# Edge blocks that begin at whole tiles: 860 tile gathers in place of 1004, groups that share tiles, and a ring of 44 places

## The chip, the cores and the metric

The kernel runs on one core of a Trainium2 chip. The time is device microseconds of one execution. TensorE (PE), VectorE (DVE), ScalarE (ACT), GpSimd (POOL) and SyncE (SP) are the core's engines; each runs its own instructions in order, and they wait for one another on semaphores.

## The reference

6250 nodes with 256 features and 100000 edges (`src`, `dst`). Three parts follow each other. The edge part is a graph attention layer, the mix part a transformer block with linear attention, and the last part a mixture of six experts of which each row takes two.

```
Wh = x @ W + b                                  # 6250 x 256
e  = leaky_relu(fs[src] + fd[dst], 0.2)         # fs, fd: Wh by a vector, one number per node
w  = softmax of e over the edges with one src
h  = relu(sum over a src's edges of w * Wh[dst])
x1 = x + linear attention of layernorm(x);  mix = x1 + W2 gelu(W1 layernorm(x1)) (1024 wide)
out = experts of the sum of both parts (router, top 2 of 6)
```

## The kernel before

The rows are cut into 50 blocks of 125 source rows (NT, R). From 0 to 440 us the kernel makes the projections and ranks the edges by block of rows (a counting sort of edges on chip); from 440 to 722 us it writes the sorted edges to `sorted_slots` in memory while the linear attention runs beside it (in `attend`), a stretch in which VectorE has the most to do. At 722 to 738 us the slots are read back (SP), turned (PE) and split by VectorE into `idx_tab`, the node to gather for each slot, and `row_tab`, its source row within the block (lines 839 to 843).

Then comes the edge loop, 738 to 2081 us. A tile is 128 edges, one per partition; a group is GT = 4 tiles, and a group's edges all belong to one block of rows. Before, each block of rows is padded to whole groups, so there are NG = 251 groups and 1004 tiles. GpSimd issues one indirect DMA per tile (line 1212), which gathers 128 rows of 258 floats (Wh and the destination term) from `wh_table` into the buffer `gath`, a ring of RG = 10 groups; it may refill a group's places when TensorE has summed it (`p_main`). Per group:

- DVE `shifted` (1234) waits for the group's gathers, `mark` (1241, four times) makes the one-hot matrix of each tile from `row_tab`, PE `turn` (1434) transposes it, DVE `group_peak` (1251) takes the maximum per row, and five operations on 125x1 numbers keep the running maximum.
- ACT `divide` (1365 to 1370) splits the new maximum into three bf16 parts, `spread` (1353) makes the transposed one-hot, PE `fetch` (1444) hands each edge its row's numbers, and DVE `score_sum`, `score_leaky`, `score_less_max` (1291 to 1305) give the exponents.
- ACT `apart` (1384, four times) and `weigh` (1393, four times) make the weights' matrix, PE `total` (1453) sums weights by gathered rows, DVE `gather_up` (1315) adds it into the block's accumulator `acc_mem` after the rescaling by ACT `rescale` (1376).

The function `together` (line 92) writes the order of every engine out by hand: a slot holds each listed stage once, for the group that lies the given number of slots back, as here for ACT and PE:

```
together(act, roots, [(3, divide), (2, spread), (3, apart), (3, rescale), (4, weigh)], feed)
together(pe, [(5, total), (3, fetch)], feed, [(0, turn), (2, load_block)])
```

Ten slots (PER) make one chunk of 250 rows of the feed-forward network, whose work (`feed`) stands in fixed slots: the sum and the layer norm's statistics on DVE in slot 0 and its root on ACT (295) in slot 1, ACT's `hidden` (1406) in slots 3 to 6, PE's `hidden` (1472) in slots 2 to 5 and `ff` (1483) in slots 6 to 9. Twenty slots are one pass of a loop. After it the experts run to the end at 2609 us.

The block number of a group is a word of the table `group_block`, which PE, DVE and ACT each load into a register once per group (1427, 1252, 1360); with it they address `own_all`, `fr_c` and the accumulator.

## Time and profile before

| | |
|---|---|
| median of 3 runs | 2607.07 us (2606.63 to 2610.53) |
| the profiled execution, its own time | 2610.57 us |
| its span | 2608.9 us |
| mean granted TensorE clock | 0.891 |
| busy over the span: PE, DVE, ACT, POOL | 2048.0, 1857.1, 1579.6, 1353.8 us |
| gathers (1212) | 1004, from 737.9 to 2051.4 us |

Busy time of the whole span mixes stages with different limits; the stretch that matters to an edit is the one in which it stands. A wait is put down to what ended it last. "Issue" is time in which an engine waited for nothing that the profile shows.

### The profile page before, as it was taken

The numbers are of one execution on the slowest core, as the hardware profiler recorded it, in microseconds if no ns is written. First come the engines' busy times: TensorE is split into PE (matmuls) and PEld (weight loads), VectorE is DVE, ScalarE is ACT, GpSimd is POOL, SyncE is SP. The second block draws the span as 40 slices with busy tenths as digits, with TensorE's granted clock in tenths as the row PEclk, the third lists the DMA queues.
The fourth block names the chain that finished last, engine by engine and source line by source line (L and its number), as shares of the span: only waits on it lengthen the run. The fifth ranks groups of instructions, "written<-read, shape, count | busy, mean of one in ns | idle before, by whom it ended". The sixth has DMA issues, their size and how long they took to land. (4 is left out here: it accounts for less than half of the span.)

```text
span 2608.9 us, 50564 instructions
## 1 busy us (share of the span) xinstructions
PE 2048.0 (79%) x10254; PEld 1601.6 (61%) x10255; DVE 1857.1 (71%) x6158; ACT 1579.6 (61%) x4950; POOL 1353.8 (52%) x1284
## 2 busy tenths in 40 slices
PE   2888666788748889888898898888888766099997
PEld 1444355677636667666676676666766556088886
DVE  7877689999856778778777787787877564044553
ACT  4666375333137778778787787787878764033332
POOL 0000000011257777777777777777777348645555
PEclk9999977999869989899899898998988866599999
DMA  4100000111133433343334333343343265435554
GB/s 144 43 27 28 18 9 19 50 24 24 20 84 107 109 107 106 107 106 109 106 106 111 107 106 106 107 110 107 106 109 103 61 177 134 116 68 92 97 93 60
DMA packets 130131, 223.37 MB, mean 86 GB/s; under 512 B 37607, under 2 KB 80660, under 8 KB 129820
## 3 DMA queue, kind: packets, MB, share of 16 engines
q0 software_dynamic: 78864, 160.18, 25.7%
q1 hardware_dynamic: 49418, 58.93, 7.8%
q14 instruction: 263, 2.15, 0.3%
q10 hardware_dynamic: 1538, 1.31, 0.2%
q8 instruction: 48, 0.79, 0.1%
HBM read 171.72 MB, written 49.77 MB: 85 GB/s over the span
## 5 line engine op out<-in xcount | busy, mean ns | idle before, releaser
L1212 POOL DMA_INDIRECT area<-wh_table,area x1004 | 1008.6, 1005 | 319.4 <-issue 303.1
L1453 PE MATMUL bank<-area 128*126 128x258 f32 x2008 | 558.4, 426 | 72.5 <-ACT area L1393 53.6
L1453 PEld LDWEIGHTS bank<-area 128*126 128x126 f32 x2008 | 397.1, 208 | 174.6 <-ACT area L1393 100.9
L512 POOL DMA_INDIRECT sorted_slots<-area x28 | 45.8, 1634 | 671.1 <-issue 486.2
L1241 DVE TENSOR_SCALAR area<-iota_row,area 128x126 f32<-128x126 f32 x1004 | 357.8, 363 | 19.4 <-issue 4.0
L1393 ACT ACTIVATE area<-area 128x126 f32<-128x126 f32 x1004 | 316.4, 388 | 49.6 <-issue 31.3
L1384 ACT ACTIVATE area<-iota_row,area 128x126 f32<-128x126 f32 x1004 | 315.7, 388 | 0.0
L1943 POOL DMA_INDIRECT out_dram<-area x108 | 169.9, 1573 | 160.1 <-DVE area L2002 143.4
L1434 PE MATMUL bank<-ident,area 128*126 128x128 f32 x1004 | 165.6, 291 | 63.3 <-DVE area L1241 61.3
L1472 PE MATMUL bank<-area 128*128 128x250 f32 x800 | 209.0, 407 | 0.0
L1483 PE MATMUL bank<-area 128*125 128x256 f32 x800 | 197.5, 390 | 0.0
L1251 DVE TENSOR_REDUCE area<-bank 125x1 f32<-125x512 f32 x251 | 171.1, 682 | 32.1 <-issue 32.1
L1315 DVE SCALAR_TENSOR_TENSOR acc_mem<-acc_mem,area,bank 125x258 f32 x251 | 121.3, 483 | 95.1 <-PE bank L1453 64.1
L1434 PEld LDWEIGHTS bank<-ident,area 128*126 128x126 f32 x1004 | 124.1, 146 | 101.2 <-DVE area L1241 52.7
L1353 ACT ACTIVATE area<-bank 125x512 bf16<-125x512 f32 x251 | 145.6, 580 | 60.9 <-DVE area L1251 60.7
L1472 PEld LDWEIGHTS bank<-area 128*128 128x128 f32 x800 | 155.4, 205 | 16.2
L1642 POOL DMA_INDIRECT moe_rows<-area x100 | 120.8, 1208 | 65.1 <-ACT area L1793 35.6
L1483 PEld LDWEIGHTS bank<-area 128*125 128x125 f32 x800 | 142.1, 187 | 16.8
L1444 PEld LDWEIGHTS bank<-own_all,area 125*128 125x128 bf16 x1004 | 52.1, 99 | 162.8 <-issue 149.3
L2002 DVE SCALAR_TENSOR_TENSOR area<-bank,area 128x256 f32<-128x256 f32 x108 | 47.4, 480 | 144.0 <-DMA out_dram<-area 80.3
L1234 DVE TENSOR_SCALAR area<-area,shift 128x4 f32<-128x4 f32 x251 | 61.7, 246 | 103.7 <-DMA area<-wh_table,area 103.6
L2034 ACT ACTIVATE area<-bank,area 128x256 f32<-128x256 f32 x108 | 45.2, 470 | 141.7 <-issue 133.7
(340 smaller groups left out, 4192.2 us busy)
## 6 DMA issues: line engine op xcount, KB each, us to landing
area<-wh_table,area POOLq DMA_INDIRECT x1004
area<-moe_rows SPq DMA_DIRECT2D x54, 264.0 KB, 2.8
wh_table<-area SPq DMA_DIRECT2D x50, 126.0 KB
xn<-in_x_dram SPq DMA_DIRECT2D x25, 250.0 KB
x_rows<-area SPq DMA_DIRECT2D x25, 250.0 KB
area<-x_rows SPq DMA_DIRECT2D x25, 250.0 KB
area<-in_L_ffn_expert_w_dram SPq DMA_DIRECT2D x3, 1536.0 KB, 11.7
out_dram<-xn SPq DMA_DIRECT2D x2, 1500.0 KB
```

The lines of the kernel that those rows point to most:

```text
L1212: g.indirect_dma_start(out=gath[:, s % RG, t, :], out_offset=None, in_=table, in_offset=bass.IndirectOffsetOnAxis(ap=idx_tab[:, s * GT + t ...
L1241: ins = V.tensor_scalar(xm[:, b, t, :], iota_row[:, :], row_tab[:, bass.ds(at(s, GT, t), 1)], fdc[:, b, t:t + 1], ALU.is_equal, ALU.mult)
L1251: V.tensor_reduce(gmax[0:R, b:b + 1], bank[XT[j % 2]][0:R, :], AX.X, ALU.max).then_inc(d_m, 1)
L1315: V.scalar_tensor_tensor(row, row, alpha[0:R, j % 5:j % 5 + 1], bank[US][0:R, 0:WROW], ALU.mult, ALU.add).then_inc(d_acc, 1)
L1353: A.activation(hot[0:R, b, :], bank[XT[j % 2]][0:R, :], ACT.Sign).then_inc(a_hot, 1)
L1384: last = A.activation(dist[:, b, t, :], iota_row[:, :], ACT.Abs, bias=row_tab[:, bass.ds(at(s, GT, t), 1)], scale=-1.0)
L1393: last = A.activation(sm[:, b, t, :], dist[:, b, t, :], ACT.Exp, bias=e3[:, b, t:t + 1], scale=-1.0e12)
L1434: last = T.transpose(bank[XT[j % 2]][0:RW, t * L:(t + 1) * L], xm[:, b, t, :], ident[:, :])
L1453: last = T.matmul(bank[US][0:RW, 0:WROW], sm[:, b, t, :], gath[:, j % RG, t, :], start=(t == 0), stop=(t == GT - 1))
L1472: last = T.matmul(bank[HB[p % 2]][:, i * CH:(i + 1) * CH], w_1[:, k, f * 128:(f + 1) * 128], x1T[:, k, :], start=(k == 0), stop=(k == 1))
L1483: last = T.matmul(bank[AB][0:R, r * D:(r + 1) * D], hT[:, f, r * R:(r + 1) * R], w_2[:, f, :], start=(f == 0), stop=(f == 7))
L1943: g.indirect_dma_start(out=out, out_offset=bass.IndirectOffsetOnAxis(ap=rowi[:, j % RB6, s, MW - 2:MW - 1], axis=0), in_=yo[:, j % 3, s, : ...
```

## The change

Blocks of rows begin at a whole tile instead of a whole group. The bound on the tiles falls from 1004 to 860 (NB = 215 blocks of four gathers), while the number of groups stays 251: a block's last group has four tiles as before, but its last tiles can be the first of the next block of rows. To keep those edges out of a group, `row_tab` carries 2^17 times the block's number, and a new ACT stage `own_rows` subtracts the group's own from its four columns into `rowl`; an edge of another block then matches no row. For the given input 234 groups hold edges, in 835 tiles; the other groups all name the last four tiles.

A group's word in `group_tab` has its first tile (bits 0 to 9), the first tile's place in the ring (10 to 15) and the block (from 16). DVE, PE and ACT each load and unpack it once per group. The ring has 44 places; since a group can begin at any place, SP copies the first three behind the last once in eleven blocks. GpSimd now waits for a semaphore `room`, that SP raises when the table's row 32 (how many groups must be summed) allows it, and the consumers wait for `ready`, that SP raises after a block's gathers. DVE's `shifted` no longer waits for the gathers but for `own_rows` (`a_row`), and ACT waits for `ready`. `mark` and `apart` read `rowl` at a fixed address instead of `row_tab` at a register's. The load of `x1` moves from SP's queue to ACT's (slot 5). The tables are 860 wide instead of 1004. In the setup VectorE has nine more small operations (50 wide) before the comparison `gcmp` and some 22 (mostly 251 wide) after it, and PE six small matmuls.

```diff
-GS, GS_BITS = GT * L, 9
-NG = (E + NT * (LO - 1 + GS - 1)) // GS
-TILES = NG * GT
-SLOTS = NG * GS
+GS = GT * L
+MOST = (E + NT * (LO - 1 + L - 1)) // L
+NG = (MOST + NT * (GT - 1)) // GT
+NB = -(-(MOST + GT - 1) // GT)
+TILES = NB * GT
+SLOTS = TILES * L
+RING = 11
+RS = RING * GT
+AHEAD = 2
+BLOCK = 2.0 ** 17
...
-                dve.wait_ge(gmap_done, 1)
-                V.tensor_scalar(group_block[:, :], bank[KV + 1][0:1, 0:NG], float(NT - 1), None, ALU.min)
+                dve.wait_ge(gmap_done, 2)
+                step(V.scalar_tensor_tensor(tf, iota_g, float(GT), bank[KV][:, 128:128 + NG], ALU.mult, ALU.add))
+                V.tensor_scalar(over, bank[KV + 1][0:1, 128:128 + NG], float(NT - 1), None, ALU.min)
...
+                step(V.scalar_tensor_tensor(word, over, 65536.0, tf[0:1, :], ALU.mult, ALU.add))
...
+                step(V.scalar_tensor_tensor(spot, whole, -float(RS), spot, ALU.mult, ALU.add))
+                V.scalar_tensor_tensor(group_tab[0:1, :], spot, 1024.0, word, ALU.mult, ALU.add)
+                dve.wait_ge(consts, 3)
+                V.tensor_scalar(tcmp, iota_t, tcol[0:NT, :], BLOCK, ALU.is_ge, ALU.mult)
...
-                V.tensor_scalar(row_tab, vrow, -1.0, None, ALU.add)
+                for i in range(-(-TILES // 512)):
+                    a, b = 512 * i, min(TILES, 512 * i + 512)
+                    V.scalar_tensor_tensor(row_tab[:, a:b], vrow[:, a:b], -1.0, bank[i][:, 0:b - a], ALU.add, ALU.add)
...
-        gath = take(RG, GT, WROW)
+        gath = take(RS + GT - 1, WROW)
...
+        def unpack(eng, word, s, first=None, place=None, blk=None):
+
+            eng.reg_load(word, group_tab[0:1, bass.ds(at(s), 1)])
+            if first is not None:
+                eng.reg_alu(first, word, 1023, ALU.bitwise_and)
+            if place is not None:
+                eng.reg_alu(place, word, 10, ALU.logical_shift_right)
+                eng.reg_alu(place, place, 63, ALU.bitwise_and)
+            if blk is not None:
+                eng.reg_alu(blk, word, 16, ALU.logical_shift_right)
...
-                load_x1((0, 2, 0), 0)
-                together(sp, feed)
+                sp.dma_start(x1[0:R, 0, :, :].rearrange("p t d -> p (t d)"), x1_rows[0:R, :]).then_inc(x1_in, 16)
+                uses = [sp.alloc_register(f"uses{i}") for i in range(2)]
+                for b in range(NB):
+                    f = b + AHEAD
+                    if RING <= f < NB:
+                        sp.reg_load(uses[f % 2], group_tab[32:33, f - RING:f - RING + 1])
+                        sp.wait_ge(p_main, sp.snap(uses[f % 2], min_val=1, max_val=NG))
+                        sp.sem_inc(room, 1)
+                    sp.wait_ge(gathered[b % RING], 16 * GT * (b // RING + 1))
+                    if b % RING == RING - 1:
+                        sp.dma_start(gath[:, RS:RS + GT - 1, :], gath[:, 0:GT - 1, :]).then_inc(repeated, 16)
+                        sp.wait_ge(repeated, 16 * (b // RING + 1))
+                    sp.sem_inc(ready, GT)
...
-                for s in range(NG):
-                    if s >= RG:
-                        g.wait_ge(p_main, s - RG + 1)
-                    for t in range(GT):
-                        g.indirect_dma_start(out=gath[:, s % RG, t, :], out_offset=None, in_=table,
+                for b in range(NB):
+                    if b >= RING:
+                        g.wait_ge(room, b - RING + 1)
+                    for i in range(GT * b, GT * b + GT):
+                        g.indirect_dma_start(out=gath[:, (i + GT) % RS, :], out_offset=None, in_=table,
...
-                    dve.wait_ge(gathered[j % RG], at((s[0], 2 * PER // RG, j // RG), 16 * GT, 16 * GT))
+                    dve.wait_ge(a_row, at(s, 1, 1))
                     wait(dve, p_xt, at(s, 1, -1))
-                    V.tensor_scalar(fdc[:, b, :], gath[:, j % RG, :, D], shift[:, :], None, ALU.add).then_inc(d_fdc, 1)
+                    V.tensor_scalar(fdc[:, b, :], dst_terms(j), shift[:, :], None, ALU.add).then_inc(d_x, 1)
...
+                def own_rows(s, j):
+
+                    unpack(act, word, s, first=firsts[j % 2], blk=blocks[j % 5])
+                    first = act.snap(firsts[j % 2], min_val=0, max_val=TILES - GT)
+                    r = act.snap(blocks[j % 5], min_val=0, max_val=NT - 1)
+                    act.wait_ge(ready, first + GT)
+                    wait(act, d_x, at(s, 2, -8))
+                    wait(act, a_dist, at(s, 1, -4))
+                    A.activation(rowl[:, j % 5, :], row_tab[:, bass.ds(first, GT)], ACT.Identity, bias=iota_blk[:, bass.ds(r, 1)]).then_inc(a_row, 1)
...
-                together(act, roots, [(3, divide), (2, spread), (3, apart), (3, rescale), (4, weigh)], feed)
+                together(act, roots, [(3, divide), (2, spread), (3, apart), (3, rescale), (4, weigh), (-1, own_rows)], feed)
...
-                        last = T.matmul(bank[US][0:RW, 0:WROW], sm[:, b, t, :], gath[:, j % RG, t, :], start=(t == 0), stop=(t == GT - 1))
+                        last = T.matmul(bank[US][0:RW, 0:WROW], sm[:, b, t, :], gath[:, bass.ds(place + t, 1), :].rearrange("p a w -> p (a w)"),
+                                        start=(t == 0), stop=(t == GT - 1))
...
-                together(pe, [(5, total), (3, fetch)], feed, [(0, turn), (2, load_block)])
+                together(pe, [(5, total), (3, fetch)], feed, [(0, turn), (2, load_group)])
```

On ACT, in a slot without parts of the feed-forward network: 1376 is `rescale`, 1393 `weigh`, 1360 to 1370 the next group's `divide`. Before:

```order
L1376 ACTIVATE area<-area 125x1 [waits d_acc,d_m]
L1393 ACTIVATE area<-area 128x126 [waits p_main,d_e,a_dist]
L1393 ACTIVATE area<-area 128x126 x3
L1360 TENSOR_LOAD group_block
L1365 ISA [waits p_q,d_m]
L1365 COPY own_all<-area 125x1
```

Now, with `rescale` at 1467, `weigh` at 1484, `own_rows` at 1248 to 1447 and `divide` from 1456:

```order
L1467 ACTIVATE area<-area 125x1 [waits d_acc,d_m]
L1484 ACTIVATE area<-area 128x126 [waits p_main,d_e,a_dist]
L1484 ACTIVATE area<-area 128x126 x3
L1248 TENSOR_LOAD group_tab
L1250 REGISTER_ALU
L1255 ISA
L1447 ISA [waits a_dist,d_x,ready]
L1447 ACTIVATE area<-area,iota_blk 128x4
L1456 ISA [waits p_q,d_m]
L1456 COPY own_all<-area 125x1
```

The load of the word has moved ahead of a new 128x4 operation, which waits for the gathers and stands between `weigh` and the next `divide`; every later instruction of ACT is behind it.

On DVE, at the border of two slots near the loop's start: 1251 is `group_peak`, 1234 `shifted`, 1241 `mark`, 1258 `row_score`. Before:

```order
L1241 TENSOR_SCALAR area<-iota_row,area 128x126 [waits d_fdc] x4
L1251 TENSOR_REDUCE area<-bank 125x1 [waits p_xt]
L1252 TENSOR_LOAD group_block
L1234 TENSOR_SCALAR area<-area,shift 128x4 [waits p_xt,gathered2]
L1258 ISA [waits d_m]
```

Now, with 1331 for `group_peak`, 1314 for `shifted` and 1321 for `mark`:

```order
L1321 TENSOR_SCALAR area<-iota_row,area 128x126 [waits d_x] x4
L1248 TENSOR_LOAD group_tab
L1252 REGISTER_ALU
L1253 REGISTER_ALU
L1255 REGISTER_ALU
L1331 TENSOR_REDUCE area<-bank 125x1 [waits p_xt]
L1307 ISA [waits p_xt,a_row]
L1314 TENSOR_SCALAR area<-area,shift 128x4
L1337 ISA [waits d_m]
```

The load stands before the maximum and is followed by three register operations, and `shifted` waits for ACT's `a_row` where it waited for the gathers.

## Rows read from the trace of the kernel before

**Rows 1.** Busy time of each engine by stretch (columns in the first row).

```profile
core 0: us, PE busy (x) PEld busy (x) DVE busy (x) ACT busy (x) POOL busy (x), PEclk, DMA share, GB/s
466.00:722.00 256.00, 209.39 (x1420) 185.40 (x1420) 231.71 (x379) 74.41 (x197) 44.21 (x27) 0.94 0.13 30
...
796.00:2054.00 1258.00, 1065.81 (x5477) 825.29 (x5475) 967.93 (x4104) 1004.25 (x3627) 963.97 (x960) 0.92 0.39 107
```

**Rows 2.** The gathers of line 1212, and what ended the idle time before them.

```profile
L1212 POOL DMA_INDIRECT area<-wh_table,area x1004: 994/998/1453, 737.9 to 2051.4; - x168
...
  issue: 303.1, 994
...
  PE bank L1453: 2.7, 9
```

**Rows 3.** Line 1234 from 796 to 2050 us.

```profile
L1234 DVE TENSOR_SCALAR area<-area,shift x240: 217/229/442, 796.8 to 2049.0; 128x4 f32<-128x4 f32 x120
...
  DMA area<-wh_table,area: 86.2, 86
```

**Rows 4.** Waits, 1321.4 to 1376.1 us: total us, times, longest.

```profile
DVE area L1234 <- DMA area<-wh_table,area: 4.9, 6, 1.3
...
DVE area L1251 <- issue: 3.3, 1, 3.3
...
PE bank L1453 <- ACT area L1393: 2.2, 5, 1.0
...
ACT area L295 <- DVE area L274: 1.7, 1, 1.7
```

**Rows 5.** ACT's order of time with hidden: start, length, line.

```profile
1402.80 1.26 ACT L1393 ACTIVATE area<-area 128x126 f32<-128x126 f32 x4
1403.95 0.81 ACT L1406 ACTIVATE area<-bank,area 128x250 f32<-128x250 f32 x2
...
1404.97 0.30 ACT L1367 ACTIVATE own_all<-own_all,area  x1
1405.17 0.28 ACT L1368 ACTIVATE area<-own_all,area 125x1 f32 x1
...
1407.41 0.19 ACT L1376 ACTIVATE area<-area 125x1 f32<-125x1 f32 x1
1407.50 0.39 ACT L1393 ACTIVATE area<-area 128x126 f32<-128x126 f32 x1
```

**Rows 6.** ACT's order of time, groups without hidden, then slot 0.

```profile
1416.92 1.26 ACT L1393 ACTIVATE area<-area 128x126 f32<-128x126 f32 x4
...
1425.20 1.26 ACT L1393 ACTIVATE area<-area 128x126 f32<-128x126 f32 x4
...
1431.77 0.30 ACT L295 ACTIVATE area<-area,eps 125x2 f32<-125x2 f32 x1 [1.30 <-DVE area L274]
```

**Rows 7.** VectorE's order of time, one group.

```profile
1407.76 0.68 DVE L1251 TENSOR_REDUCE area<-bank 125x1 f32<-125x512 f32 x1
...
1411.65 0.69 DVE L1251 TENSOR_REDUCE area<-bank 125x1 f32<-125x512 f32 x1
```

**Rows 8.** Sequencer instructions at line 1360 (ACT): length min/median/max in ns.

```profile
L1360 ACTq TENSOR_LOAD <-group_block x251: 273/278/487, 754.1 to 2066.1; - x126
L1360 ACTq FUSED_REGOPS  x209: 42/43/43, 856.4 to 1992.7; - x105
```

**Rows 9.** VectorE's order of time in the setup.

```profile
461.26 0.21 DVE L778 TENSOR_TENSOR acc_mem<-acc_mem,ident 128x50 f32<-128x50 f32 x1
461.50 0.21 DVE L779 TENSOR_REDUCE acc_mem<-acc_mem 128x1 f32<-128x50 f32 x1
...
466.13 0.40 DVE L793 TENSOR_SCALAR group_block<-bank 1x251 int32<-1x251 f32 x1
```

**Rows 10.** VectorE between the tables and the loop.

```profile
736.20 0.68 DVE L843 TENSOR_SCALAR area<-acc_mem 128x1004 f32<-128x1004 int32 x1
...
739.97 10.81 DVE L1220 MEMSET acc_mem<- 128x12900 f32 x1 [2.64 <-issue]
```

More of the change, by code:

```diff
@@ L44 @@
 PER = 10
-RG = 10
 LAG = 5
@@ L325, in gps_kernel @@
         vrow = take(TILES).bitcast(I32)
+        tcmp, iota_t = take(TILES)[0:NT, :], take(TILES)[0:NT, :]
+        tf = take(NG)
+        spot, whole, over = (take(NG)[0:1, :] for _ in range(3))
+        word = take(NG)[0:1, :]
+        turns = take(NG)[0:1, :].bitcast(I32)
+        rcmp = take(2, NB)
         XB, QB, HEADS, NUM, DEN, OUT = 0, 1, 2, 3, 4, 5
@@ L1449, in total @@
                     b = j % 2
+                    place = pe.snap(places[j % 4], min_val=0, max_val=RS - 1)
                     pe.wait_ge(a_s, at(s, 1, 1))
```

168 lines of the change are left out of this document (108 added, 60 removed).

## The prediction

> **What bounds the kernel now.** I read the stretches first. The loop has 1258 us of the 2609 between 796 and 2054 us alone, and no engine is full there: PE 1065.8, ACT 1004.3, DVE 967.9, POOL 964.0 us [rows 1]. A busy share below 85% for all four means either waits in a circle or time that isn't counted as busy. So the second view is that of the gathers. They take 998 ns each, 1004 of them from 737.9 to 2051.4 us, and the idle time between them is "issue" in 994 cases, 303.1 us; GpSimd waited for a free place 9 times, 2.7 us in all [rows 2]. One gather is thus followed by the next at (2051.4 - 737.9 - 2.7) / 1003 = 1.307 us whatever the others do, 5.23 us for a group of four. Line 1234, the first consumer, goes from 796.8 to 2049.0 us in 239 steps, 5.24 us each [rows 3]: the loop runs at GpSimd's pace.
>
> By how much? The consumer waits for the gathers 86 times of 240, 86.2 us in all [rows 3]. Without these waits it would need 1252.2 - 86.2 = 1166.0 us, 4.88 a group. In a stretch with few such waits, 1321.4 to 1376.1 us, 4.9 us of it in 6 waits, the other waits show: ACT's root of slot 1 waits 1.7 us for DVE's statistics, PE 2.2 us for ACT's weights, and DVE stands 3.3 us at the loop's jump [rows 4]. The compute side is a second bound 7% under the first, and it is a chain: in the slots with `hidden`, ACT goes from one `weigh` to the next in 1407.50 - 1402.80 = 4.70 us with no gap at all [rows 5], in the others in (1425.20 - 1416.92) / 2 = 4.14 us [rows 6], and then waits 1.30 us before the root in slot 1 [rows 6]. DVE needs 1411.65 - 1407.76 = 3.89 us for a group without feed-forward work [rows 7].
>
> **The change, part by part.** The sum is made against the profiled execution's 2610.57 us, which is 3.5 us above the median of the three runs.
>
> *Fewer gathers.* 144 of 1.307 us are 188 us of GpSimd's time. That is no gain by itself: 860 gathers take 1124 us, over 251 groups 4.48 us, over the 234 groups that hold edges (835 tiles) 4.66. Both are below the 4.88 of the compute side, so GpSimd stops being the bound, and what can be won is the waits: -86.2 us. The one rule of the Trainium skill that bears on this (Perfetto Trace Analysis, "What 'DMA-bound' means") says that a kernel can be bound on the sequencer that issues its DMAs, where its track is solid slices, and that such a window is the making of descriptors and not the movement of data. The trace agrees, with 994 gaps of 0.30 us between 1004 slices. By that rule alone the kernel would scale with the number of gathers; that is the first rival below.
>
> *ACT's new operation.* `own_rows` is one ACTIVATE of 128x4. No such shape is in the trace. The nearest are the 125x1 ones: 1405.17 - 1404.97 = 0.20 us from start to start, and 0.09 for 1376 before `weigh` [rows 5]; from below 0.09, from above the 0.30 of a single one that someone waits for [rows 5]. I take 0.20. Its place is between `weigh` and the next `divide`. In the four slots with `hidden`, where ACT has no gap, it costs in full: 0.8 us per ten groups. In slots 7 to 9 PE with `ff` and ACT share the chain, and I count it in full again, 0.6. In slot 0 DVE's `shifted` now stands behind ACT: before, DVE was about a slot ahead of ACT and its only wait was for data that lay in the ring; now it waits for an operation that ACT does after `weigh` of the slot before, and `feed_sum` and the statistics, for which ACT waits 1.30 us anyway [rows 6], stand behind that. I take 1.0 us per ten groups (below: 0, if DVE's lead isn't used; above: the 1.3 again). Together 2.4 us per ten groups, 24 times: +57.6 us, 0.24 us a group.
>
> *Loads and register work.* ACT's TENSOR_LOAD is 278 ns and a register operation 43 [rows 8]. `own_rows` has one load, as `divide` had, but two more register operations and one more waiting instruction, 0.1 us in ACT's sequencer. The load stood between two ACTIVATEs before, while the four `weigh` operations still ran (1.26 us, [rows 5]); their length covers it. If it stops being covered, since the wait for `ready` needs the loaded value, it costs 0.28 to 0.4 us a group; that is a rival. On DVE the three register operations come before the maximum instead of behind it, and `mark` loses a register operation each: I count DVE's own balance as nothing, since DVE has 4.88 - 3.89 = 1 us of room in most slots [rows 7]. On PE the load was there, and two register operations run ahead behind 2 us of matrix work. SP's part, `ready` after a block and a copy of three places once in eleven, lies beside all engines, as the ring holds eleven blocks.
>
> *The waits that come next.* With the gathers gone as a pace-setter, PE's wait for ACT's weights (2.2 us in ten groups, [rows 4]) can grow in slots 6 to 9. I count +5 us for the loop. The 17 groups at the end name the last block of tiles, which GpSimd may fetch only when group 229 or so is summed; the consumers are only five groups behind and have to wait once for about a group's gathers: +5 us (one gather time of 5.2 us; below 0).
>
> *Setup.* DVE is busy 231.7 of 256 us between 466 and 722 us [rows 1], so what it gets there is paid. The nine small steps go at the pace of 461.50 - 461.26 = 0.24 us [rows 9]: +2.2. Of the others those of 1x251 are like 793 (0.40 long, [rows 9]), those of one column like the 0.24; 22 of 0.26 are +5.8. If all of it fell into DVE's 24 idle us it would be 0; if each took 0.40 it would be 11. I take +8. Three operations on the tables, 0.68 us each [rows 10], become a seventh narrower, -0.3, and the loop can start about 1 us sooner or later, as it waits for the memset of `acc_mem` that stands 2.64 us after its predecessor and takes 10.81 [rows 10]: -1.
>
> Sum: -86.2 + 57.6 + 5 + 5 + 8 - 0.3 - 1 = -11.9 us, from 2610.57 to 2598.7 in a like execution, 2595 as a median.
>
> **The rivals.**
> 1. *`own_rows` is hidden.* If ACT's 0.20 us fits into gaps (it is 80% busy in the loop, 1004.3 of 1258, [rows 1]), the 57.6 us fall away: 2595 - 57.6 = 2538 us. Against it: the slots without a gap. Chance 0.17, and most of it for a part, near 2550.
> 2. *The full gain.* The time scales with the gathers: 2607 - 188 + 8 = 2427 us. It needs a compute side below 4.48 us a group, and a slot with `hidden` takes 4.70 by itself [rows 5]. It is what the rule of the Trainium skill named above would give. Chance 0.03.
> 3. *Slower: the coupling.* ACT's load, its two register operations and its wait stand in the chain `weigh`, `own_rows`, `shifted`, `mark`, `turn`, `group_peak`, `divide`, so each group pays 0.28 + 0.09 beside the 0.20. For the ten slots with the load in the open that is 0.57 - 0.24 = 0.33 us more a group, 240 times: +79, 2674 us; in the four `hidden` slots alone 0.37 x 96 = +36, 2631. It decides from (86.2 - 5 - 5 - 6.7) / 240 = 0.29 us a group. For it: the load's value is now needed at once, by a wait. Against it: `weigh`'s 1.26 us lie over it. Chance 0.26.
> 4. *The ring or `room` holds the gathers back,* because SP waits in turn for sums, gathers and copies, so the loop stays at 5.24 us: 2607 + 8 - 10 = 2605 us. Against it: the ring is eleven blocks deep, and GpSimd waited 2.7 us in all with ten [rows 2]. Chance 0.07.
>
> **How the numbers follow.** The forecast has 0.47, its own range is 2560 to 2612 (`own_rows` at 0.09 and 0.30 us, setup 0 to 11, slot 0 at 0 and 1.3). The range of 2545 to 2640 leaves out the full gain, about half of the first rival below 2545, and the upper part of the third, 0.11. A measurement of this kernel tells about 0.2% from no change, 5.2 us. Faster by more: 0.34 of the forecast's 0.47, 0.17, 0.03 and 0.03 of the ring's: 0.57. Within it: 0.09, 0.04 of the coupling and 0.03: 0.16. Slower: 0.04, 0.22 and 0.01: 0.27.
>
> **What would show it.** 860 gathers, with waits of GpSimd for SP or PE of some tens of us: it is no longer the bound. `shifted` (1314) waits for ACT's 1447 and for no DMA. From one `weigh` (1484) to the next in a `hidden` slot 4.9 us; 5.1 or more says rival 3, 4.7 rival 1. The loop from about 747 us, its stretch 1234 us long against 1252. DVE 8 us longer up to the tables. The prediction is wrong if the 1447 costs ACT over 0.3 us, if its coupling slows slots that have no `hidden`, or if the setup's operations are paid at more than their own length.

## The result, and the profile after

The changed kernel takes 2635.55 us (median of 4 runs, 2633.59 to 2638.28), the kernel before beside it 2608.8 us (4 runs). The ratio is 1.0097 with a 95% interval of 1.0084 to 1.0111: 1% slower, where 0.5% faster was forecast. The profiled execution has a span of 2634.5 us against 2608.9, 25.6 us more.

From the page of the changed kernel, the groups of the gathers (1282), of `weigh` (1484) and of `group_peak` (1331), with busy time, mean ns of one, and the idle time before them:

```profile
L1282 POOL DMA_INDIRECT area<-wh_table,area x860 | 872.0, 1014 | 395.6 <-issue 248.8
...
L1484 ACT ACTIVATE area<-area 128x126 f32<-128x126 f32 x1004 | 316.2, 387 | 20.6 <-DVE area L1384 18.3
...
L1331 DVE TENSOR_REDUCE area<-bank 125x1 f32<-125x512 f32 x251 | 172.6, 688 | 82.3 <-issue 75.1
```

The gathers by themselves, with what ended the idle time before them, answer to [rows 2]:

```profile
L1282 POOL DMA_INDIRECT area<-wh_table,area x860: 992/998/1511, 754.2 to 2007.6; - x172
...
  issue: 248.8, 816
  SPq L1267: 133.7, 43
```

860 gathers went out, and GpSimd waited 133.7 us for SP's `room`, where it had waited 2.7 us for a free place. It is not the bound any more. That step of the prediction is right. The first consumer, `shifted`, was to wait for ACT and no transfer [rows 3]:

```profile
L1314 DVE TENSOR_SCALAR area<-area,shift x251: 220/230/481, 768.2 to 2083.0; 128x4 f32 x126
...
  ACT area L1447: 81.2, 126
  issue: 19.8, 11
```

The busy time by stretch, with the columns of [rows 1]:

```profile
466.00:722.00 256.00, 213.66 (x1384) 188.03 (x1384) 237.06 (x413) 75.53 (x199) 39.73 (x24) 0.92 0.13 30
...
796.00:2054.00 1258.00, 1061.18 (x5417) 821.43 (x5416) 927.63 (x4060) 1033.39 (x3821) 839.87 (x828) 0.91 0.36 99
```

ACT rose from 1004 to 1033 us of 1258, DVE fell from 968 to 928, and PE is the fullest with 84%: the loop is a chain, now a longer one. The chain's waits in the loop (total us, times, longest), to be read beside [rows 4]:

```profile
DVE area L1331 <- issue: 73.3, 153, 3.5
DVE area L1314 <- ACT area L1447: 73.0, 121, 4.5
ACT area L301 <- DVE area L280: 65.0, 24, 3.1
PE bank L1555 <- ACT area L1484: 64.6, 136, 1.5
...
DVE area L1314 <- issue: 18.8, 10, 2.1
```

The first and the last of these are stops that no other engine explains. Their counterparts in the kernel before:

```profile
DVE area L1251 <- issue: 32.1, 10, 3.4
...
DVE area L1294 <- issue: 14.4, 10, 1.7
```

VectorE stopped like this ahead of `group_peak` only at the loop's ten jumps before, and stops there 153 times now. The second line is a stop just behind the jump, 1.4 us on the mean; now it comes ahead of `shifted` (1314) and is 1.9. Both return below.

To see where the 25.6 us are, I take `weigh` as a clock: it runs once per group in both kernels, four instructions each time. Its row in the view by line gives the ns of one (least, median, most) and the first and last start. Of the kernel before:

```profile
L1393 ACT ACTIVATE area<-area x1004: 382/387/402, 767.1 to 2074.4; 128x126 f32<-128x126 f32 x168
```

And of the changed one:

```profile
L1484 ACT ACTIVATE area<-area x1004: 382/387/400, 787.2 to 2104.5; 128x126 f32<-128x126 f32 x168
```

| stretch, us | before | changed | difference |
|---|---|---|---|
| start to first gather [rows 2] | 737.9 | 754.2 | +16.3 |
| first gather to first `weigh` | 29.2 | 33.0 | +3.8 |
| first to last `weigh`, 251 groups | 1307.3 | 1317.3 | +10.0 |
| last `weigh` to the end | 534.5 | 530.0 | -4.5 |

The loop has lost its bound and is 10 us longer. The pace between the 40th and the 230th group is 5.213 us before and 5.312 now.

### The profile page after: what moved, and what is told of

Read it like the earlier page. It is cut to its first block and busy times, and to the rows that moved or that the text cites. A ratio compares the mean times of both kernels' runs of the same rounds, so it can differ in the third digit from the quotient of the medians.

```text
span 2634.5 us, 53974 instructions
## 1 busy us (share of the span) xinstructions
PE 2068.0 (78%) x10267; PEld 1614.9 (61%) x10268; DVE 1835.9 (70%) x6190; ACT 1623.0 (62%) x5201; POOL 1218.4 (46%) x1141
## 5 line engine op out<-in xcount | busy, mean ns | idle before, releaser
L1282 POOL DMA_INDIRECT area<-wh_table,area x860 | 872.0, 1014 | 395.6 <-issue 248.8
L1555 PE MATMUL bank<-area 128*126 x2008 | 563.0, 428 | 80.5 <-ACT area L1484 68.5
L1545 PE MATMUL bank<-own_all,area 125*128 x1004 | 63.5, 168 | 105.7 <-ACT own_all L1461 51.9
```

Of the source, the lines that this page charges most:

```text
L1282: g.indirect_dma_start(out=gath[:, (i + GT) % RS, :], out_offset=None, in_=table, in_offset=bass.IndirectOffsetOnAxis(ap=idx_tab[:, i:i + ...
L1555: last = T.matmul(bank[US][0:RW, 0:WROW], sm[:, b, t, :], gath[:, bass.ds(place + t, 1), :].rearrange("p a w -> p (a w)"), start=(t == 0), ...
```

## The experiments

All kernels below carry one small edit in the last part of the program, which the two controls carry alone. "Loop" is the time from the first to the last `weigh`, "pace" the mean over the 190 groups from the 40th to the 230th; the ratio is to the kernel before on the same chip.

| kernel | us | ratio | 95% interval | loop | pace |
|---|---|---|---|---|---|
| c_before | 2612.68 | 1.0001 | 0.9988 to 1.0013 | 1307.5 | 5.214 |
| c_after | 2635.7 | 1.0097 | 1.008 to 1.0114 | 1318.8 | 5.321 |
| b_half_gathers | 2549.39 | 0.9768 | 0.9752 to 0.9784 | 1249.0 | 5.023 |
| a_no_activate | 2591.32 | 0.9923 | 0.9907 to 0.994 | 1277.3 | 5.140 |
| a_two_slots_ahead | 2616.19 | 1.0029 | 1.0017 to 1.004 | 1296.8 | 5.223 |
| a_rows_on_dve | 2624.15 | 1.0056 | 1.0039 to 1.0073 | 1313.6 | 5.285 |
| a_half_gathers | 2632.9 | 1.0089 | 1.0072 to 1.0105 | 1314.6 | 5.295 |
| b_more_setup | 2621.86 | one run | | 1310.3 | 5.236 |
| a_ahead_no_activate | 2598.82 | 0.9955 | 0.9939 to 0.9972 | 1275.7 | 5.139 |
| a_four_on_dve | 2576.45 | 0.987 | 0.9844 to 0.9895 | 1254.9 | 5.034 |
| a_six_on_dve | 2588.12 | 0.9921 | 0.9903 to 0.994 | 1273.7 | 5.094 |
| a_eight_loads | 2637.34 | 1.0102 | 1.0084 to 1.012 | 1318.5 | 5.320 |
| a_ahead_eight_loads | 2615.98 | 1.002 | 1.0003 to 1.0036 | 1295.5 | 5.217 |
| b_half_loads | 2552.79 | 0.9778 | 0.9761 to 0.9796 | 1248.9 | 5.023 |
| b_half_memsets | 2561.04 | 0.8674 | 0.8629 to 0.8719 | 1241.1 | 4.961 |
| a_eight_memsets | 2932.09 | 0.9928 | 0.9897 to 0.996 | 1593.4 | 6.523 |
| a_ahead_eight_memsets | 2922.49 | 0.9922 | 0.9886 to 0.9959 | 1594.5 | 6.518 |
| a_eight_memsets_2 | 2926.06 | 0.9928 | 0.9896 to 0.9961 | 1581.3 | 6.492 |

In the last four rows the kernel before took 2951.3 or 2948.35 us beside them and not some 2610, so their ratios can't be set beside the others (more on this at the memsets).

### The two controls

```diff
-                            dve.reg_load(reg, clear[0:1, j:j + 1])
+                            dve.reg_load(raw_clear, clear[0:1, j:j + 1])
+                            dve.reg_alu(reg, raw_clear, 0, ALU.max)
```

> The kernel before with one small edit in its last part: the two counts that VectorE loads and waits against there pass through a maximum with 0. All kernels of this study carry it, so this is their reference. The edit adds some 200 register operations after the loop. Expected: 2607 to 2617 us, the loop unchanged, 5.21 us a group.

> The changed kernel with the same small edit, and with SP's loaded count passed through a maximum with 1. Expected: 2634 to 2645 us. It also tells which of the 16.3 us by which the first gather came later belong to the change: 8.3 us are VectorE's added operations; 3.2 us had arisen before 165 us, where the change adds nothing. If these 3.2 us are an accident of one execution, the first gathers of the two kernels here lie 13 us apart; if they belong to the kernel, 16.

The edit costs nothing that can be measured, and the change is worth +0.97% a second time. The setup is the point here. The last operation ahead of anything that the change adds there and the first one behind it stand in the kernel before (776 and 821) and in the changed one (784 and 859) at other times. VectorE's order of time in the kernel before:

```profile
460.98 0.24 DVE L776 TENSOR_SCALAR area<-area 128x28 int32<-128x28 f32 x1
...
466.55 0.64 DVE L821 MEMSET area<- 128x308 uint32 x2
```

In the changed one, where 811 and 831 are two of those added:

```profile
464.38 0.24 DVE L784 TENSOR_SCALAR area<-area 128x28 int32<-128x28 f32 x1
...
472.46 0.41 DVE L811 SCALAR_TENSOR_TENSOR acc_mem<-area,bank 128x251 f32<-128x251 f32 x1
...
477.58 0.65 DVE L831 TENSOR_SCALAR acc_mem<-acc_mem 50x860 f32<-50x860 f32 x1
478.24 0.64 DVE L859 MEMSET area<- 128x308 uint32 x2
```

Between the two VectorE needed 5.57 us and now 13.86: the added operations cost 8.3 us, as forecast (8). But 464.38 - 460.98 = 3.4 us of delay were there already, where nothing is added. In c_before the same place came 3.1 us later than in the kernel before (464.07), whose code it shares up to there, and in c_after 5.1 us earlier (455.84): this part is an accident of the execution. The first gather of c_after is at 745.6 us, that of c_before at 740.9. Counted from that place, the first gather comes 276.9 us later in the kernel before and in c_before, and 289.8 in the changed kernel and in c_after: +12.9 both times, the 8.3 and another 4.6.

### The kernel before with half its gathers

```diff
-                    for t in range(GT):
+                    for t in range(GT if s < RG else 2):
...
-                    dve.wait_ge(gathered[j % RG], at((s[0], 2 * PER // RG, j // RG), 16 * GT, 16 * GT))
+                    dve.wait_ge(gathered[j % RG], at((s[0], 2 * PER // RG, j // RG), 32, 64))
```

> The kernel before, but from the eleventh group on only two of a group's four tiles are gathered (the other two places keep old rows; all else is computed as before). GpSimd then needs 2.6 us a group and can't be the bound. Theory of the prediction: VectorE's 86 us of waits for gathers are all on the path, so the loop takes 4.88 us a group and the time is 2520 us. Theory now: VectorE runs up to a slot ahead of ACT, which has no gap in four slots of ten, so half of its waiting was slack; the compute side needs 47.95 us for ten groups, and about 5.1 more where the loop jumps, 5.05 us a group, so the time is about 2567 us.

The row of `weigh` in this kernel:

```profile
L1393 ACT ACTIVATE area<-area x1004: 383/388/402, 770.5 to 2019.5; 128x126 f32<-128x126 f32 x168
```

The loop is 58.3 us shorter, the time 61.6. It lies between the two theories, 2520 and 2567 us: the pace is 5.02, near the 5.05 of the second one, but the first forty groups gain another 15 us and the last twenty 7. The prediction's 86.2 us were the sum of what one instruction waited. VectorE runs ahead of ACT by up to a slot, and in the steady part none of its waiting falls in the first ten groups of a pass and most of it (43 us) in the last four; 51 us of waiting between the 40th and the 240th group were worth (5.213 - 5.023) x 200 = 38 us.

### Without the ACTIVATE

```diff
-                    A.activation(rowl[:, j % 5, :], row_tab[:, bass.ds(first, GT)], ACT.Identity, bias=iota_blk[:, bass.ds(r, 1)]).then_inc(a_row, 1)
+                    act.sem_inc(a_row, 1)
```

> The changed kernel without the ACTIVATE of own_rows: load, register operations, the wait for ready and the release of VectorE stay, rowl is filled once before the loop (so the edges' rows are not the right ones). Theory now: the operation's 0.20 us are paid in every slot, since ACT has no gap there, so the loop falls by 0.20 us a group to 5.11 and the time to about 2588 us; ten groups of the first half of a pass take 48.8 us instead of 50.75, of which slot 0 keeps its 0.96. Rival: the price is the coupling of VectorE to ACT and the load in front; then the loop stays at 5.25 to 5.31 us a group and the time within 10 us of the changed kernel.

2591.32 us, 44.4 less than c_after, where the theory said about 2588: the operation's own time on ACT is what is paid, and not the load in front of it. A slot with `hidden` of the changed kernel shows the price (start, length, line; [rows 5] is the same slot before):

```profile
1425.34 1.26 ACT L1484 ACTIVATE area<-area 128x126 f32<-128x126 f32 x4
1426.50 0.29 ACT L1447 ACTIVATE area<-area,iota_blk 128x4 f32 x1
1426.69 0.81 ACT L1497 ACTIVATE area<-bank,area 128x250 f32<-128x250 f32 x2
...
1430.25 0.68 ACT L1484 ACTIVATE area<-area 128x126 f32<-128x126 f32 x2
```

`own_rows` (1447) starts at 1426.50 and the next operation at 1426.69: 0.19 us, and from one `weigh` to the next it is 1430.25 - 1425.34 = 4.91 us where it was 4.70. The forecast had 0.20 and 4.9.

### own_rows two slots ahead, or on VectorE

Two slots ahead is one number, with `rowl` and the registers made tenfold:

```diff
-                together(act, roots, [(3, divide), (2, spread), (3, apart), (3, rescale), (4, weigh), (-1, own_rows)], feed)
+                together(act, roots, [(3, divide), (2, spread), (3, apart), (3, rescale), (4, weigh), (-2, own_rows)], feed)
```

> The changed kernel with own_rows two slots ahead instead of one (rowl and the registers tenfold). Nothing is left out. Theory: VectorE's shifted no longer waits for an operation that ACT does just before, so the coupling's part (0.12 us a group: 0.5 in slot 0, 0.45 two slots later, 1.5 where the loop jumps) goes, the 0.20 us on ACT stay: 5.20 us a group, about 2607 us. Rival: the excess in these slots comes from ACT's own added instructions and not from the wait; then nothing changes, 5.32 us a group and 2635 us.

In a_rows_on_dve the operation leaves ACT and stands before `shifted`:

```diff
-                    dve.wait_ge(a_row, at(s, 1, 1))
+                    first = dve.snap(firsts[j % 2], min_val=0, max_val=TILES - GT)
+                    dve.wait_ge(ready, first + GT)
+                    wait(dve, a_dist, at(s, 1, -4))
+                    V.tensor_scalar(rowl[:, j % 5, :], row_tab[:, bass.ds(first, GT)], iota_blk[:, bass.ds(block_of(j), 1)], None, ALU.add).then_inc(a_row, 1)
```

> The changed kernel with own_rows on VectorE: VectorE loads the first tile with the place and the block, waits for ready and makes rowl itself ahead of shifted; ACT only loads the block's number before divide, as before the change. Nothing is left out. Theory (ACT's 0.20 us in every slot, 0.18 a group, and the coupling of VectorE to ACT, 0.12 a group): both fall away, VectorE has about 1 us of room in most slots, and the loop comes to 5.02 to 5.08 us a group, the time to about 2570 us. Rival: VectorE's chain from shifted over the marks is what the loop pays, and 0.25 us and a wait more there cost as much as on ACT: 5.2 us a group or more, 2605 us or more.

One slot of lead is worth 22.0 us of the loop (1318.8 to 1296.8) and 19.5 of the time. The slot in which ACT waits for the feed-forward statistics falls from 7.42 to 6.42 us; the prediction had 1.0 for it. As much again comes from the slot with the jump (8.64 to 7.66 us).

All ten on VectorE miss the expectation of 2570 us by 54. ACT's slots with `hidden` are back at 4.71 us, but VectorE, in order of time over two groups, can't follow (1339 is `group_peak`, 1318 the new operation):

```profile
1301.44 0.68 DVE L1339 TENSOR_REDUCE area<-bank 125x1 f32<-125x512 f32 x1
1302.04 0.22 DVE L1318 TENSOR_SCALAR area<-area,iota_blk 128x4 f32 x1
...
1305.70 0.69 DVE L1339 TENSOR_REDUCE area<-bank 125x1 f32<-125x512 f32 x1 [0.29 <-PE bank L1531]
1306.31 0.26 DVE L1318 TENSOR_SCALAR area<-area,iota_blk 128x4 f32 x1
...
1309.93 0.69 DVE L1339 TENSOR_REDUCE area<-bank 125x1 f32<-125x512 f32 x1 [0.28 <-issue]
```

From one `group_peak` to the next it now takes 1309.93 - 1305.70 = 4.23 us where [rows 7] have 3.89. Ten of these and the feed work of slots 0 and 2 leave no room: in slot 0 ACT waits until 8.5 us lie between two `weigh`. My "1 us of room" was true of a slot without feed and not of ten slots.

### Is anything left of the gather bound, and what does the setup cost?

> The changed kernel, but from the twelfth block on only two of its four tiles are gathered (the other places keep old rows). Theory: GpSimd is no bound of the changed loop, so its pace stays at 5.31 to 5.32 us a group between the 40th and the 230th; only the loop's filling gets shorter, by up to 8 us: 2627 to 2635 us. Rival: ready and room hold the loop back somewhere, and the pace falls by more than 0.05 us a group, under 2622 us.

The edit is that of b_half_gathers, from the twelfth block on. 2632.9 us, and 5.295 us a group against 5.321: at most 0.03 a group is left of the gathers, so the last of the prediction's rivals, that the ring or `room` holds the loop back, is out. The setup is tried on the kernel before:

```diff
+                for _ in range(6):
+                    step(V.tensor_tensor(tmp50, gend, ident[:, 0:NT], ALU.mult))
+                    step(V.tensor_reduce(gcol, tmp50, AX.X, ALU.add))
...
+                for _ in range(13):
+                    step(V.tensor_scalar(group_block[:, :], bank[KV + 1][0:1, 0:NG], float(NT - 1), None, ALU.min))
```

> The kernel before with 12 more of VectorE's 50-wide operations ahead of the comparison gcmp and 12 more of the 1x251 one after it (the same values again, so nothing changes): 12 x 0.245 + 12 x 0.42 = 8.0 us of VectorE's time, without the changed kernel's six matmuls. Theory: what VectorE gets there is paid at its own length, 8 us between the projections' end and the first gather. Rival: it is paid at more, as in the changed kernel, where the stretch from 445 us to the first gather grew by 12 to 13 us.

The first gather is at 749.2 us, 11.3 later than before the change, of which 0.7 us had arisen at 776 (461.67): 10.6 us for operations that took 8.3. What VectorE gets there is paid at its own length and a little more. The stretch behind them differs between executions (in b_half_gathers, whose program is that of c_before there, it took 3.2 us longer), so the little more isn't settled.

### What is left: two kernels that should not differ so

```diff
+                    if j % 10 in OWN:
+                        unpack(act, word, s, blk=blocks[j % 10])
+                        return
```

> The changed kernel with own_rows two slots ahead and without its ACTIVATE (rowl is filled once, so the edges' rows are not the right ones); loads, register work and semaphores stay. It closes the account: with the coupling (0.09 to 0.12 us a group) and the operation (0.18 to 0.20) both gone, the pace should be that of the kernel before with half its gathers, 5.02 us a group, and the time 2611 - 58 (no gather to wait for) + 12 (setup) = 2565 to 2572 us. If load, register work, dynamic places and the loop's longer code cost something of their own, the pace stays above 5.06.

> The kernel with own_rows two slots ahead, but for the four groups of ten whose turn falls in ACT's slots with hidden (3 to 6) VectorE makes rowl itself, in its slots 5 to 8, where it has no feed work. Nothing is left out. Theory: ACT's slots with hidden go back from 4.91 to 4.71 us, VectorE's 0.2 to 0.3 us in its four slots are hidden: 5.22 - 0.08 = 5.14 us a group, 2616 - 19 = 2597 us, faster than both kernels. Rival: VectorE has no room (all ten on it gave 5.285), so the first half of a pass stays at 49.8 us or more and the time at 2611 us or more.

> The same with six of ten groups on VectorE, in its slots 4 to 9. Theory: ACT saves 0.2 us in six slots, 5.10 us a group and about 2588 us, if VectorE's room in these six slots is 0.3 us each; between no move and ten there is a best number. Rival: VectorE loses the lead that it needs in slot 0 for the feed-forward sum, and slot 0 grows by more than the two further slots save; then it is slower than with four.

The lines shown are ACT's in a_four_on_dve (OWN is 5, 6, 7, 8) and a_six_on_dve (4 to 9): for these groups only the block is unpacked there, and `shifted` does the rest as in a_rows_on_dve. a_four_on_dve takes 2576.45 us, 1.3% less than the kernel before and 59 us less than the change, with nothing left out. Its row of `weigh`:

```profile
L1506 ACT ACTIVATE area<-area x1004: 382/388/400, 786.7 to 2041.6; 128x126 f32<-128x126 f32 x168
```

It does better than its theory by 20 us. a_ahead_no_activate has both earlier edits, the two slots of lead and no ACTIVATE, and is worse than expected by 27 us or more: 5.139 us a group, no better than without the ACTIVATE one slot ahead. The two don't fit together with prices per operation alone. Their traces tell where the time is; the table has medians over the ten passes from the 40th to the 240th group, in us from one `weigh` to the next (the second and third row from the middle of a pass):

| slot | b_half_gathers | c_after | a_two_slots_ahead | a_no_activate | a_ahead_no_activate | a_four_on_dve |
|---|---|---|---|---|---|---|
| with `hidden` | 4.71 | 4.91 | 4.91 | 4.71 | 4.71 | 4.71 |
| with ACT's wait for the statistics | 6.38 | 7.42 | 6.42 | 6.91 | 6.90 | 6.32 |
| two slots later | 6.20 | 6.47 | 6.47 | 6.67 | 6.67 | 6.07 |
| with the jump | 6.74 | 8.64 | 7.66 | 8.29 | 8.35 | 5.98 |
| all twenty | 100.8 | 106.5 | 104.6 | 103.1 | 103.2 | 100.9 |

Where ACT has no gap, the operation costs its 0.20 us and no more. With the operation gone, three slots in which ACT waits for VectorE are longer than in a_two_slots_ahead, which does more work: ACT, being faster, only waits for longer. So once ACT's part is gone the loop goes by VectorE, and the lead adds nothing (1277.3 and 1275.7 us of loop). VectorE's own pace shows it. In groups where it has no feed work, from one `group_peak` to the next, in b_half_gathers:

```profile
1318.98 0.69 DVE L1251 TENSOR_REDUCE area<-bank 125x1 f32<-125x512 f32 x1
...
1322.85 0.68 DVE L1251 TENSOR_REDUCE area<-bank 125x1 f32<-125x512 f32 x1
```

And the same group in a_ahead_no_activate, where `group_peak` is 1334:

```profile
1351.54 0.69 DVE L1334 TENSOR_REDUCE area<-bank 125x1 f32<-125x512 f32 x1 [0.20 <-PE bank L1539]
...
1355.49 0.69 DVE L1334 TENSOR_REDUCE area<-bank 125x1 f32<-125x512 f32 x1 [0.20 <-issue]
```

That is 3.95 us where it was 3.87, with 0.20 us of idle time ahead of the maximum, where the load of the word and its three register operations now stand; other groups of this kind went from 3.82 to 4.02 and from 3.84 to 3.91. The rest is where the loop jumps. The next three are VectorE's order of time there, and each begins with `gather_up`, the last operation ahead of the jump (1315, 1394, 1413). The kernel before:

```profile
1371.69 0.48 DVE L1315 SCALAR_TENSOR_TENSOR acc_mem<-acc_mem,area,bank 125x258 f32 x1 [0.17 <-issue]
1375.43 0.69 DVE L1251 TENSOR_REDUCE area<-bank 125x1 f32<-125x512 f32 x1 [3.25 <-issue]
1376.06 0.23 DVE L1234 TENSOR_SCALAR area<-area,shift 128x4 f32<-128x4 f32 x1
1376.26 0.18 DVE L1291 TENSOR_REDUCE area<-bank 128x8 f32<-128x24 f32 x1
1377.95 0.16 DVE L1294 TENSOR_TENSOR area<-area 128x4 f32<-128x4 f32 x1 [1.51 <-issue]
```

The changed kernel:

```profile
1392.66 0.48 DVE L1394 SCALAR_TENSOR_TENSOR acc_mem<-acc_mem,area,bank 125x258 f32 x1 [0.17 <-ACT area L1467]
1396.47 0.69 DVE L1331 TENSOR_REDUCE area<-bank 125x1 f32<-125x512 f32 x1 [3.33 <-issue]
1399.26 0.23 DVE L1314 TENSOR_SCALAR area<-area,shift 128x4 f32 x1 [2.10 <-issue]
```

The kernel a_four_on_dve:

```profile
1365.20 0.48 DVE L1413 SCALAR_TENSOR_TENSOR acc_mem<-acc_mem,area,bank 125x258 f32 x1 [0.35 <-PE bank L1578]
1369.08 0.69 DVE L1350 TENSOR_REDUCE area<-bank 125x1 f32<-125x512 f32 x1 [3.40 <-issue]
1369.69 0.22 DVE L1331 TENSOR_SCALAR area<-area,shift 128x4 f32 x1
```

All three stand 3.3 to 3.4 us at the jump. The kernel before then stops again for 1.5 us ahead of 1294, the changed one for 2.1 us ahead of `shifted` (its longest; the means of ten passes are 1.4 and 1.9), a_four_on_dve not at all. With VectorE's instructions counted in the order of the records, the second stop is at the 2110th or 2111th in the kernel before and at the 2238th or 2239th in the changed one, in every pass; the loops begin at 2099 and 2234. In a_no_activate and a_ahead_no_activate the loop begins one instruction later and the stop comes one instruction sooner in it, so it belongs to a place in the code and not to an instruction. In a_four_on_dve, a_six_on_dve and b_more_setup the loops begin at 2270, 2288 and 2123, in a_rows_on_dve at 2330, and there is no second stop. One queue brings code in the changed kernel from 1000 to 2000 us (packets, MB, share of the engines):

```profile
q14 instruction: 179, 1.47, 0.5%
```

That is 8.2 KB a packet; in the trace they are of 8192 bytes. I took the stop for code that arrives in pieces, whose borders are 128 instructions apart, and tried to move the loop (eight loads; fourteen in the kernel before with half its gathers):

```diff
+                for _ in range(8):
+                    dve.reg_load(word, group_tab[0:1, 0:1])
```

> The changed kernel with eight more register loads on VectorE ahead of the loop, which do nothing but move the loop's code by eight instructions. In each pass of the loop of the changed kernel VectorE stands about 3 us at the jump and, 4 instructions after it, another 2.1 to 2.5 us, which no semaphore explains; in the kernel before it is 1.4 to 1.6 us, 11 instructions after it, and in the three kernels whose loop begins elsewhere in the code there is no second stop within 60 instructions. Counted in VectorE's recorded instructions these second stops are at 2110 and at 2238: 128 apart. Theory: code arrives in pieces of 128, and a loop that begins just ahead of a border waits twice. Here the loop begins behind the border: the second stop goes, the pace falls from 5.32 to about 5.21 us a group, the time from 2635.7 to about 2610 us. Rival: the 2 us are a wait for ACT; then the stop and the time stay.

> The same eight loads in the kernel with own_rows two slots ahead. With the second stop gone as well only ACT's operation is left of the change's price in the loop: pace 5.22 to 5.12 us a group, time 2616 to about 2592 us. If the coupling is what the eight loads remove, this kernel changes by less than 5 us.

> The kernel before with half its gathers and fourteen loads on VectorE ahead of the loop, which take the loop's beginning over its border. It tells what the kernel before's own second stop (1.5 us a pass) was worth where no gather hides it: pace 5.023 to 4.95 to 4.98 us a group, time 2549 to 2535 to 2542 us; if the stop is hidden by VectorE's lead, it stays at 2549 us.

Nothing moved. The loop's jump stood at the same count as without the loads, so they are not in the built program, and the three runs are repeats: 2637.34, 2615.98 and 2552.79 us against 2635.7, 2616.19 and 2549.39. They show how well such numbers repeat, 0.1%. Memsets stay (eight, or fourteen in the third), in the setup:

```diff
+                for _ in range(8):
+                    step(V.memset(tmp50[:, 0:1], 0.0))
```

> The register loads of the last runs aren't in the built program (VectorE's first jump stands at the same count of instructions, 3194, as without them), so those three kernels repeat the ones they came from. Here the code is moved by eight memsets of one column in the setup, which stay: 0.1 to 0.2 us each, about 1 to 2 us in all. Theory of code that arrives in pieces of 128: the second stop at VectorE's fourth instruction after the jump goes, the pace falls from 5.32 to about 5.21 us a group, the time from 2636 to about 2612 us. Rival: stop, pace and time stay (2637 us).

> The same eight memsets in the kernel with own_rows two slots ahead: without the second stop 5.12 us a group and about 2593 us; if the stop is no matter of the code's place, 5.22 and 2617 us.

> The kernel before with half its gathers and fourteen such memsets: VectorE's loop begins behind the border. 5.023 falls to 4.95 to 4.98 us a group and 2551 to about 2540 us if the stop of 1.5 us a pass was on the path, else 2551 to 2554 us.

> The changed kernel with the eight memsets once more. In the last runs the kernel before took 2951 us against 2608 to 2612 in all others, so the gathers landed later there and hid what was asked; VectorE's second stop after the jump was gone in all three. Theory: with gathers as in the other runs the kernel without the stop takes 5.21 us a group and about 2612 us, equal to the kernel before within 0.3%. Rival: the stop is hidden in the changed kernel, and it stays at 5.32 us a group and 2637 us.

In all four the second stop is gone from every pass. VectorE's order of time in a_eight_memsets, with `gather_up` (1398), the jump, `group_peak` (1335) and `shifted` (1318):

```profile
1410.44 0.48 DVE L1398 SCALAR_TENSOR_TENSOR acc_mem<-acc_mem,area,bank 125x258 f32 x1 [0.18 <-issue]
1414.16 0.69 DVE L1335 TENSOR_REDUCE area<-bank 125x1 f32<-125x512 f32 x1 [3.24 <-issue]
1414.77 0.22 DVE L1318 TENSOR_SCALAR area<-area,shift 128x4 f32 x1
1414.90 0.17 DVE L1374 TENSOR_REDUCE area<-bank 128x8 f32<-128x24 f32 x1
```

What it is worth in the changed kernel these runs can't say. Beside them the kernel before took 2951.3 and 2948.35 us instead of some 2610, and the kernels with all gathers 2932.09, 2922.49 and 2926.06 (ratios 0.9928, 0.9922 and 0.9928), at 6.5 us a group. The last expectation puts this down to gathers that land later, and the traces say otherwise: in a_eight_memsets GpSimd waits 464.1 us for `room`, which follows PE's sums, where it waited 133.7, so the gathers are not what the loop waits for. It isn't the chip alone either: the first three ran on the chip numbered 8, a_eight_memsets_2 on the one numbered 2, where c_before had taken 2612.68 us. The changed kernel with the memsets is 0.7% faster than the kernel before there, while without them it is 1% slower elsewhere. What held these runs up stays open.

b_half_memsets, with half the gathers, had the same trouble only at the start. Its waits from 755 to 810 us, of engines that no instruction in the view had held up, beside that for gathers:

```profile
PEld bank L1446 <- issue: 23.6, 3, 19.3
DVE area L1253 <- remote: 20.3, 2, 11.3
...
DVE area L1236 <- DMA area<-wh_table,area: 4.1, 2, 3.0
```

The first `weigh` comes 45.6 us after the first gather instead of 29.0, and the whole takes 2561.04 us, more than b_half_gathers with 2549.39. From there on it runs as elsewhere and gains: a loop of 1241.1 against 1249.0 us, 4.961 against 5.023 us a group, 1.2 us a pass. In the medians of the slots only two differ by more than 0.1 us: the one with the jump (6.05 against 6.74 us) and the one behind it (7.36 against 8.06). So the gain stands where the stop was, although the two kernels didn't run side by side.

## Why the prediction was wrong

**What bounds the kernel** was right. GpSimd's gathers did, and after the change they don't.

**"What can be won is the waits: -86.2 us"** is the step that failed first. The kernel before with half its gathers wins 58.3 us in the loop. The wait of one instruction is not the gain of its engine's chain where that engine runs ahead of another: 28 us of the 86 were slack. This is three quarters of the distance from the forecast (-11.9 us) to the measurement (+25.6).

**ACT's operation and the coupling, +57.6 us,** had the right mechanism. Against the loop without a gather bound (1249.0) the changed one needs 1317.3: +68.3. Of the 1318.8 of c_after the operation is 41.5 (0.20 us in each of 240 groups would be 48) and one slot more of lead 22.0; the sizes of 0.20 for the operation and 1.0 for slot 0 are what the trace shows. They don't add up: with both gone the loop is 1275.7, 43.1 shorter and not 63.5. By that reading the 57.6 were not too small but too large, and what is missing is the next term.

**"I count DVE's own balance as nothing"** failed as well. With both causes gone the loop is still 26.7 us longer than that of b_half_gathers. By the table above that is 2.4 us a pass: 1.6 in the slot with the jump and 1.4 in three other slots in which ACT waits for VectorE, less 0.7 in the rest. In the first lie a longer stand at the jump (a mean of 3.6 us ahead of `group_peak` against 2.7) and a longer second stop; in the others VectorE's pace of 3.91 to 4.02 us a group against 3.82 to 3.87, which the load and the register operations ahead of the maximum lengthen. That these are the causes is read from the traces; no run takes them away one by one in the changed kernel.

**The waits that come next, +5 and +5,** were not there as such: the last twenty groups took no longer than before. The sum of what the loop was to lose comes out right all the same, 57.6 + 5 + 5 = 67.6 us against 68.3, but that is luck: it is made of other parts.

**The setup, +8,** was right for VectorE's operations (8.3). What was missed are 4.6 us between them and the first gather, the same in both pairs, and 3.8 us in the filling of the loop, where I had -1.

Put together: -58.3 + 68.3 + 8.3 + 3.8 - 4.5 = +17.6 us, and 3.4 us of the profile's 25.6 are an accident ahead of the edit; the rest are the 4.6 us between VectorE's added operations and the first gather, whose cause is open. A stretch of this length differed by up to 4.3 us between executions of kernels with the same work there.

**The rivals.** The full gain, the second of the list (the working calls it the first), is out: with 522 gathers the kernel before still takes 2549.39 us, so GpSimd's issue was the bound only down to there. The third, the coupling, was closest in its result (2631 to 2674), but not in its reason: the load's time isn't paid in the slots with `hidden`, which take the 4.91 us of the forecast and not 5.1. Its point of decision, 0.29 us a group, had been worked out from the 86.2. With 58.3 it is (58.3 - 6.7) / 251 = 0.21 us, and the change costs 68.3 / 251 = 0.27. The profile of the kernel before could have told: ACT is solid in four slots and VectorE a slot ahead of it [rows 5 to 7], so a wait of VectorE for a gather delays the loop only after that lead is used up.

## What to carry to other kernels

To price the removal of a bound, run the kernel with the bound taken away, here with half the gathers left out, before the edit is written: one such run gives -58 us where the sum of waits said -86. When work has to be added to a loop of coupled engines, put it slot by slot where an engine has room, and ahead of its consumer by more than one slot. The same 128x4 operation cost 40 us on ACT everywhere; two slots of lead gave back 20 us. With four of ten moved to VectorE the kernel gained another 40 us, but not all by the move: the eight slots with `hidden` give back 1.5 us a pass, and the slot with the jump 1.7 us, about as much as the second stop, which this kernel doesn't have because its loop begins elsewhere in the code. So nearly half of its gain is in all likelihood luck of place: 1.7 us in twelve passes are the 20 us by which its expectation was missed. Price an engine's room over the whole period, not in one slot, and before comparing two loops look whether both stop behind the jump.

## What the runs showed of the hardware

A jump back to the loop's start costs VectorE 2.6 us (b_half_gathers) to 3.9 us (a_six_on_dve), and a loop whose start lies just ahead of a certain border in the code stops again 3 to 11 instructions later, for 1.2 to 2.5 us, once 3.3; eight or fourteen instructions ahead of the loop remove that. The two borders that were seen, in two different programs, are 128 recorded instructions apart. The Trainium skill (Runtime: NRT & Kernel Launch, "Instruction fetch mechanics") says that code is refilled in blocks of 16 KiB, 256 instructions, while the current one runs, that this is mostly hidden, and that a taken branch to code outside the two blocks held waits for the fetch. The stand at the jump agrees with the last. The second stop agrees with blocks, but not with 256: at the page's 16 KiB for 256 instructions a packet of 8192 bytes holds 128 of them, which is an estimate, and that is the distance of the two borders. Nor was it hidden: b_half_memsets gained 1.2 us a pass of twenty groups. Where the gathers were the bound it was: b_more_setup, which has no second stop, keeps the pace of 5.236 us.

In the runs with memsets the loop with all gathers took 6.5 us a group while the loop with half of them took 4.96; GpSimd's own time for a gather was the same there, 1.002 us as the median against 0.998, and GpSimd was waiting for PE's sums. What held the engines up there isn't known.
